# Moving y's copy back on ACT behind two decays, the z convolution's taps to one per step, and the output projection over two steps, in the state-space stage of a fused kernel

## The reference

```python
x = x + 0.5 * ffn(layernorm(x))          # 16 routed experts + 2 shared, of which 4 are chosen for a token
x = x + attn(layernorm(x))               # the block of this case
x = x + 0.5 * ffn(layernorm(x))

def attn(h):
    xz = transpose(h @ W_in)             # (batch, 256, 512); x, z = its halves of 128 channels
    x = gelu(conv4(x, K_x) + b_x)        # depthwise, four taps
    z = gelu(conv4(z, K_z) + b_z)
    dt, B, C = split(x @ W_xproj, [8, 24])       # 8 + 16 + 16 columns
    delta = softplus(dt @ W_dt + b_dt)
    # 16 states of every channel, over the 512 tokens one after the other:
    h = exp(delta * A) * h + delta * B * x
    y = sum over the 16 states of h * C, plus x * D
    return concat(y, z) @ W_out
```

## Time and profile before

| What | Value |
|---|---|
| Median of 3 runs | 879.94 us (879.92 to 880.79) |
| The profiled execution | 881.1 us, of which the span of its instructions is 879.1 us |
| Granted TensorE clock, mean | 0.994 |
| PE busy over the span | 842.9 us (96%) |
| DVE busy | 700.3 us (80%) |
| POOL, ACT busy | 629.0 us (72%), 556.5 us (63%) |
| DVE busy in the stretch 334 to 567 us (state-space stage) | 223.68 of 233 us |
| PE, POOL, ACT busy in the same stretch | 208.60, 182.60, 176.76 us |

### The profile page before, as it was taken

The page is one execution under the profiler, slowest core; times in us unless marked ns, Lnnn a source line. Parts: engine busy times, 40 slices in busy tenths (PEclk is TensorE's granted clock), DMA queues, the critical chain, the costliest instruction groups (busy, mean ns, idle before and its releaser), DMA issues. The chain is left out here.

```text
span 879.1 us, 12640 instructions
## 1 busy us (share of the span) xinstructions
PE 842.9 (96%) x3851; PEld 638.1 (73%) x3851; DVE 700.3 (80%) x1279; ACT 556.5 (63%) x1048; POOL 629.0 (72%) x471
## 2 busy tenths in 40 slices
PE   8999999999999999889898996999999999999997
PEld 7678778877877785566565554687887888788885
DVE  6969768777976578999999999877977877786664
ACT  6665655565557669878888784365565556555554
POOL 7959676766766767768886996865767667676765
PEclk9999999999999999999999999999999999999999
DMA  8733574363434343444344444345457435436440
GB/s 213 227 114 107 154 192 120 115 154 123 135 105 124 104 129 119 158 142 157 120 171 144 134 148 145 122 132 162 112 164 198 128 116 144 159 108 183 141 121 24
DMA packets 125139, 122.40 MB, mean 139 GB/s; under 512 B 59272, under 2 KB 82960, under 8 KB 125072
## 3 DMA queue, kind: packets, MB, share of 16 engines
q1 hardware_dynamic: 102368, 116.35, 43.9%
q10 hardware_dynamic: 22704, 5.25, 2.8%
HBM read 112.40 MB, written 9.18 MB: 138 GB/s over the span
## 5 line engine op out<-in xcount | busy, mean ns | idle before, releaser
L806 POOL TENSOR_TENSOR act_lo<-act,act_hi 128x512 fp32r<-128x512 f32 x288 | 372.4, 1298 | 187.4 <-ACT act_hi L917 185.4
L910 ACT ACTIVATE bank<-bank 128x512 f32<-128x512 f32 x252 | 146.6, 582 | 234.1 <-PE bank L1245 222.8
L1141 DVE TENSOR_TENSOR sg<-bank,c_ring 128x512 f32<-128x512 f32 x252 | 172.6, 685 | 97.1 <-ACT bank L910 95.1
L1241 PE MATMUL bank<-x_parts,w_hi 128*128 128x512 f32 x572 | 231.4, 405 | 3.1 <-DVE sg L1141 2.0
L1119 DVE SCALAR_TENSOR_TENSOR act<-sg,bank 128x512 f32<-128x512 f32 x288 | 197.9, 687 | 40.9 <-PE bank L1245 20.5
L1242 PE MATMUL bank<-x_parts,w_lo 128*128 128x512 f32 x572 | 226.2, 395 | 0.0
L1245 PE MATMUL bank<-x_parts,w_hi 128*128 128x512 f32 x572 | 226.2, 395 | 0.0
L917 ACT ACTIVATE act_hi<-act 128x512 fp32r<-128x512 f32 x286 | 178.1, 623 | 0.4 <-PE bank L1217 0.4
L1241 PEld LDWEIGHTS bank<-x_parts,w_hi 128*128 128x128 f32 x572 | 107.5, 188 | 35.2 <-issue 4.8
L1245 PEld LDWEIGHTS bank<-x_parts,w_hi 128*128 128x128 f32 x572 | 107.5, 188 | 25.9
L1242 PEld LDWEIGHTS bank<-x_parts,w_lo 128*128 128x128 f32 x572 | 107.6, 188 | 25.7 <-issue 1.7
(11 more groups left out here) (181 smaller groups left out, 959.1 us busy)
## 6 DMA issues: line engine op xcount, KB each, us to landing
c_ring<-c_dram SPq DMA_DIRECT2D x252, 256.0 KB, 3.7
c_ring<-c_dram SPq DMA_DIRECT2D x64, 512.0 KB, 3.7
y_dram<-out_t SPq DMA_DIRECT2D x56, 64.0 KB, 2.8
y_tok<-y_dram SPq DMA_DIRECT2D x14, 256.0 KB, 3.7
xt_dram<-xn ACTq DMA_DIRECT2D x40, 64.0 KB, 3.4
xt<-xt_dram ACTq DMA_DIRECT2D x10, 256.0 KB, 2.9
out<-x_sb SPq DMA_DIRECT2D x7, 256.0 KB, 2.4
x_sb<-in_L_attn_hidden_states SPq DMA_DIRECT2D x3, 512.0 KB, 6.5
```

Source lines behind the costliest of these rows:

```text
L806: self.nc.gpsimd.tensor_tensor(m["act_lo"][:, g % LAG], m["act"][:, g % ACTS], m["act_hi"][:, g % LAG].bitcast(FP32), ALU.subtract).then_i ...
L910: nc.scalar.activation(self.h_bank[:, g % 2], self.h_bank[:, g % 2], ACT.Silu).then_inc(self.sg_ready, 1)
L1141: nc.vector.tensor_tensor(m["sg"][:, g % 2], silu, weight, ALU.mult).then_inc(self.w_done, 1)
L1241: nc.tensor.matmul(dst, m["w_hi"][:, k, n, :], x_hi, start=True, stop=False)
```

## The change

It has three edits, all in the state-space stage. ACT: at n = 4 the two decays of pair g + 2 now stand before the copy of the turned-back y, not behind it. PE: for i = 1 to 5 the z taps stand at n = 3, 4, 5, 6, one at each, where taps 1 and 2 stood together at n = 5. PE: for i = 1 to 5 and 7 the projection of sequence i - 1 is issued as two token tiles at n = 5 and two at n = 6; `out_ready` is counted up by the last tile, so at n = 6. The projection at i = 6 stays whole.

```diff
--- before.py
+++ after.py
@@ -1608,10 +1608,10 @@
                     self.act_delta(ae, i + 1)
                 if n == 3 and i:
                     (self.act_turned_y if i - 1 in TURNED else self.act_y)(ae, i - 1)
+                if RING <= g + 2 < ALL_PAIRS:
+                    self.act_decays(ae, g + 2)
                 if n == 4 and i - 1 in TURNED:
                     self.act_back_y(ae, i - 1)
-                if RING <= g + 2 < ALL_PAIRS:
-                    self.act_decays(ae, g + 2)
                 if n == 4 and i + 3 < BATCH:
                     self.norm.act_apply(ae, BATCH + i + 3)
                 if n == 6 and i and i != BATCH - 2:
@@ -1888,10 +1888,10 @@
                     if step == 3:
                         pe.wait_ge(self.delta_ready, i + 2)
                         self.pe_conv(pe, i, 1, [0] if i else [0, 1], self.z_bank(i))
-                    if n == 5 and i:
-                        self.pe_conv(pe, i, 1, [1, 2], self.z_bank(i))
-                    if n == 6:
-                        self.pe_conv(pe, i, 1, [3] if i else [2, 3], self.z_bank(i))
+                    if n in (4, 5, 6) and i:
+                        self.pe_conv(pe, i, 1, [n - 3], self.z_bank(i))
+                    if n == 6 and i == 0:
+                        self.pe_conv(pe, i, 1, [2, 3], self.z_bank(i))
                 if i == BATCH - 2:
                     if n == 1:
                         pe.wait_ge(self.rows_copied, 2 * BATCH)
@@ -1906,11 +1906,13 @@
                 if n == 3 and i - 1 in TURNED:
                     need(pe, self.xt_copied, min(i + 3, BATCH))
                     self.pe_turn_back(pe, i - 1)
-                if n == (6 if i == BATCH - 2 else 5) and i:
-                    if i == BATCH - 2:
-                        pe.wait_ge(self.z_gated, BATCH)
+                if n == 6 and i == BATCH - 2:
+                    pe.wait_ge(self.z_gated, BATCH)
                     need(pe, self.xt_copied, min(i + 3, BATCH))
                     self.pe_project_out(pe, i - 1, range(TT))
+                if n in (5, 6) and i and i != BATCH - 2:
+                    need(pe, self.xt_copied, min(i + 3, BATCH))
+                    self.pe_project_out(pe, i - 1, range(TT // 2) if n == 5 else range(TT // 2, TT))
                 if n == 6 and i + 3 < BATCH:
                     need(pe, self.x_added, i)
                     self.norm.pe_transpose(pe, BATCH + i + 3, self.misc)
```

## The result

| | before | after |
|---|---|---|
| Median of 5 runs | 879.92 us (879.39 to 880.79) | 884.55 us (883.79 to 884.84) |
| Profiled execution, its span | 881.1, 879.1 us | 884.84, 883.0 us |
| First scan to last scan | 334.66 to 564.33 | 334.87 to 567.57 |
| DVE busy over the span | 700.3 us | 699.9 us |
| PE busy over the span | 842.9 us | 843.2 us |

The ratio is 1.0049, with a 95% interval of 1.0036 to 1.0062: slower by 4.6 us. The engines do the same work in the same busy time. Between first and last scan lie 232.70 us instead of 229.67.

What follows compares the result with a forecast made beforehand. DVE was taken to bound the state-space stage (busy 223.68 of 233 us). Sequences 2 and 3 +2.20, 1 and 4 -0.52, 5 and 6 +1.57 gave +3.25 on 879.94: 883.2 us, range 880.9 to 886.0.

Steps and rivals of the forecast that it cites:

- The chain on ACT, its slack and its price: ACT from act_x to next sequence's step-2 decays: 1.43 us later, 0.33 slack, scan waits 1.10 us in sequences 1 to 4.
- The half projection at 1.30 us: PE steps 5 and 6: 12 of 24 projection instructions take 1.30 us, by the trace's 108 ns each.
- The waits for PE that go: DVE's waits for PE's spread in sequences 1, 4 and 5 vanish: 1.36 + 1.36 + 0.98 us.
- Sequence 5 into 6: Step-2 scan of sequence 6 starts 1.17 us later, the 0.98 us won in sequence 5 already spent.
- The 0.40 us behind it in sequence 6: PE's wait for ACT's copy of y passes partly to DVE: middle of 0 to 0.79 us.
- The sum for the stage: Sequences 2 and 3 +2.20, 1 and 4 -0.52, 5 and 6 +1.57: together +3.25 us.
- two falls won back: PE's clock falls in step 5 of sequences 1 and 4 no longer delay DVE: -2 x 1.36 us.
- the case without any (+5.97): If unprofiled runs had no clock fall, 2 x 1.36 us is not won: +5.97 us, 885.9.
- three places in sequences 1 to 6 where the beat is broken: DVE's 3.50 us scan beat breaks only in sequences 1, 4 and 5, 3.7 us in all to win.
- (a): Rival: PE's load is levelled, ACT's chain keeps pace, all three DVE breaks vanish: -3.7 us, 876.2; chance 0.12.
- (b): Rival: about half the step-2 scan wait is real, 0.5 us per sequence: -0.2 us, 879.7; chance 0.13.
- (c): Rival: clock falls at PE's step 0, delaying ACT's softplus about 0.8 us, 1 to 4 times: 884.0 to 886.4; chance 0.15.

Runs made afterwards that it cites:

- three doses: Changed kernel with the projection's second half ahead of the last z tap, 880.12 us; changed kernel itself, 884.55 us; kernel before with the split projection alone, 890.0 us.
- the longer chain: Kernel before, PE untouched, first part of the row moments on ACT moved from step 5 to behind act_x at step 6: 884.62 us against 880.41.
- both pieces ahead: Changed kernel with second part of the moments and front piece L586 of the second feed-forward block put ahead of act_x on ACT: 879.21 us against 880.41.
- the taps with both pieces ahead: Kernel before with one z tap per step, projection whole, second part of moments and front piece L586 ahead of act_x: 878.21 us against 880.41.
- the repeats: Kernel before, unchanged, traced twice more for its clock: spans 878.9 and 876.7 us, against 879.1 in the first trace.

## Why the prediction was right, and where it was off

The forecast was 883.2 us, slower by 3.25 us; measured were 884.55 and 4.63 us, inside the range. Its steps:

- **The chain on ACT, its slack and its price.** Forecast: `act_x` 1.43 us later, slack 0.33, wait 1.10. Measured: 7.38 - 6.04 = 1.34 us later, slack 0.33 by three doses and by the longer chain, break 1.00 in each of four sequences. Nearly all of the 0.09 us too much are the two half projections, put at 1.30 each. The handover read from the earlier trace rows (ready at 399.41, scan at 399.46) was enough to see that there was hardly any slack.
- **The half projection at 1.30 us.** The first half took 410.93 to 412.19, 1.26 us for 12 instructions or 105 ns each. The 81 ns of the Trainium skill ("TensorE: Matmul & The Clock Gate", "Back-to-back issue gap") would have given an estimated wait of 0.68 us; this case's trace does not agree with it (105 ns, and a break of 1.00 us), and the row was the better guide.
- **The waits for PE that go.** Forecast: all three. They went.
- **Sequence 5 into 6.** Forecast +1.17 net of the 0.98 won; measured 2.13 - 1.00 = +1.13.
- **The 0.40 us behind it in sequence 6** was the middle of 0 to 0.79; measured 0.65, so a middle without a row behind it was 0.25 us short. Two traces bear on the mechanism: with both pieces ahead 0.58 us stayed though the break at step 2 was 0.43, and with a lead of 0.34 us left to ACT (the taps with both pieces ahead) 0.24 us came. So 0.58 us are ACT's missing lead at the copy of y, and PE's slack took 0.21 us of the 0.79, not half. In the changed kernel's own trace PE does not wait for that copy: it runs without a gap from 510.12 on, behind the fall of the clock, and comes to L1779 only at 521.58. That this is the other 0.07 us is argued, not tested.
- **The sum for the stage.** By the same two traces: 4 x 1.00 + 2.13 + 0.65 - 1.36 - 1.35 - 1.00 = +3.07; the stage is 232.70 - 229.67 = 3.03 us longer. Forecast 3.25. The span grew by 3.9 us: 0.21 us lie before the first scan, and about 0.66 in the last feed-forward stage, where PE has the same work. These two I did not foresee and did not explain; between the traces of the kernel before the same two stretches differ by up to 1.3 and 0.45 us.
- **The term that was off: how many falls of the clock the median run has.** I charged two falls won back, 2 x 1.36, to a median that lay 1.16 us below the trace with two falls. The text gave the case without any (+5.97); the repeats show that one is usual. 3.25 + 1.36 = 4.61 us, against 4.63 measured. That is an account from five traces of the kernel before or of its PE order, since I have the falls from traces only. The agreement to 0.02 us is in part luck: the waits of 1.10 for 1.00 and the 0.40 for 0.65 lean against each other, and the 0.87 us outside the stage are in no term.
- **A misreading that cost nothing.** The prediction counts three places in sequences 1 to 6 where the beat is broken. There is a fourth, in sequence 6 from step 6 to 7 (5.35 us, so 1.85), where DVE does pieces of the second block's preparation and waits for nobody. It is the same in every trace here.
- **The rivals.** That the chain keeps pace (a) and that half of the wait is real (b) fell with the four waits of 1.00 us. The clock at a new place (c) was real in one place of this trace (sequence 6) and cost less than the 0.8 us that I gave it: `act_x` to decays took 515.08 - 504.71 = 10.37 us there, 0.07 more than the 10.30 that a chain without a wait has (10.61 - 0.31), since the clock fell at 511.31, when `pe_bc` was done, and ACT's table load and its two copies ran meanwhile. In the split alone it cost 0.26 us where it fell at 395.45, again behind `pe_bc`, and 0.97 us where it fell at 484.19, as `pe_bc` began. The argument against (c), idle times of 1.43 us at most, held for sequences 2 to 5 (1.40 or 1.41 us, no fall); the fall came at the border of sequences 5 and 6, where the idle time was 1.94 us.

The change is two edits that pull against each other. The taps at one per step win 2.1 us. Splitting the projection wins nothing on top, since the tap moved already gives DVE its spread in time, and puts step 6's spread and sum between the two halves, in front of the one semaphore that ACT's chain hangs on. The best kernels here are those with the projection whole and the taps at one per step: the taps alone take 0.9976 (0.9966 to 0.9987) of the kernel before.

## What to carry to other kernels

Splitting work on an engine that is not the bound can delay whatever its last piece signals; follow that signal through the engine that waits for it, to the next instruction of the bound, and measure the slack there before splitting. A gapless run on a second engine that ends a few tenths of a microsecond before its reader (0.38 us here, 0.05 of it the handover) is almost a bound already, even if no row shows a wait. If the signal can't come earlier, take out of the chain behind it what doesn't depend on it: the idle time in front of the wait (4.31 us here) had room for 1.8 us of moments, where 1.04 us had not.

## What was not expected of the hardware

The clock of TensorE is not the same in each run of the same program. In five traces with the same order on PE it fell from 1.00 to 0.50 (2.4 to 1.2 GHz) in step 5 of sequences 1 to 4 two, one, one, one and no times, each time for 3.4 us and behind an idle time of 1.86 to 1.88 us. That idle time does not decide it alone: PE idles 1.72 to 1.89 us at that place in each of the four sequences, and mostly no fall came, nor did one in the trace of the split alone, which has 1.87 and twice 1.72 us there. With 0.86 us of it filled by a tap, the clock fell there in none of six traces; with so few falls in the other six (five in all), that the tap is the cause is likely but not shown.
